# Attention and feed-forward block on one core: the first loads in one queue's order, six warming matmuls for eight, and two consecutive tokens to a row of a pair

## What is computed

```
x = x + softmax(q k^T / 8) v Wo + bo     q = layernorm(x) Wq, k = ctx Wk, v = ctx Wv; 8 heads of 64
y = silu((layernorm(layernorm(x)) * gamma + beta) W1 + b1)      W = (q - 128) * scales, groups of 128 rows
x = x + 0.5 * (y W2 + b2)                W1: 256 x 1024, W2: 1024 x 256
```

## Time and profile before

| | us |
|---|---|
| median of 3 runs | 188.02 (187.6 to 189.53) |
| profiled execution, its own time | 187.78 |
| its span | 186.0 |
| TensorE busy (matmul) | 180.9 |
| VectorE, ScalarE, GpSimd busy | 123.7, 123.2, 115.2 |

### The profile page before, as it was taken

One profiled execution on the slowest core, in us unless ns is written; L12 is line 12 of the kernel. 1 busy time (PEld: TensorE's weight loads), 2 busy tenths in 40 slices (PEclk: granted clock), 3 DMA queues, 4 the chain that ended last, 5 costly groups with the idle time before them and its releaser, 6 DMA issues.

```text
span 186.0 us, 3887 instructions
## 1 busy us (share of the span) xinstructions
PE 180.9 (97%) x1502; PEld 177.0 (95%) x1502; DVE 123.7 (67%) x261; ACT 123.2 (66%) x230; POOL 115.2 (62%) x159
## 2 busy tenths in 40 slices
PE   7999999899999999999999999999999999999994
PEld 7899789799999999999999999999999999999994
DVE  0189987999999374955496558847694768154341
ACT  3278752897967970898278935895289817962580
POOL 5021798997996984198708972597349762776220
PEclk9999999999999999999999999999999999999999
DMA  6998793000001000010001000100001000100101
GB/s 145 299 394 237 232 386 119 2 2 0 4 2 35 25 0 0 4 57 0 4 0 56 4 0 0 33 30 0 4 0 56 0 4 0 56 4 0 56 4 56
DMA packets 9480, 10.72 MB, mean 58 GB/s; under 512 B 2268, under 2 KB 8183, under 8 KB 9335
## 3 DMA queue, kind: packets, MB, share of 16 engines
q1 hardware_dynamic: 8981, 9.83, 16.3%
q10 hardware_dynamic: 482, 0.66, 1.3%
HBM read 8.38 MB, written 2.10 MB: 56 GB/s over the span
## 4 chain that ended last, share of the span: by engine, by line
PE 90%; DVE 6%; ACT 2%; issue 1%; POOL 0%
PE H L873 24%; PE T L887 21%; PE T L855 15%; PE S L834 14%; PE S L841 4%; PE S L784 4%; PE S L762 2%; DVE hT_hi L636 1%; PE T L817 1%; PE T L769 1%; PE H L769 1%; PE H L803 1%; PE S L803 1%; DVE smax L589 1%; DVE probs L596 1%; DVE hT_lo L638 1%
## 5 line engine op out<-in xcount | busy, mean ns | idle before, releaser
L315 POOL TENSOR_TENSOR y_lo<-y,y_hi 128x512 fp32r<-128x512 f32 x28 | 37.9, 1373 | 2.3 <-ACT y_hi L455 1.9
L873 PE MATMUL H<-hT_hi,w_hi 128*128 128x256 f32 x128 | 36.9, 288 | 0.8 <-DVE hT_lo L638 0.7
L281 POOL TENSOR_TENSOR probs<-probs,rsum 128x616 f32<-128x616 f32 x16 | 19.2, 1218 | 29.8 <-DVE rsum L608 29.8
L887 PE MATMUL T<-w_hi,y_hi 128*128 128x256 f32 x128 | 36.5, 285 | 0.0
L873 PE MATMUL H<-hT_lo,w_hi 128*128 128x256 f32 x128 | 35.5, 277 | 0.0
L873 PE MATMUL H<-hT_hi,w_lo 128*128 128x256 f32 x128 | 35.4, 277 | 0.0
L887 PE MATMUL T<-w_lo,y_hi 128*128 128x256 f32 x128 | 35.4, 277 | 0.0
L887 PE MATMUL T<-w_hi,y_lo 128*128 128x256 f32 x128 | 35.4, 276 | 0.0
L451 ACT ACTIVATE y<-H,vec 128x256 f32<-128x256 f32 x64 | 26.6, 469 | 7.0 <-PE H L873 7.0
L424 ACT ACTIVATE probs<-probs,rstd 128x616 f32<-128x616 f32 x16 | 12.8, 808 | 22.9 <-DVE probs L596 22.9
L873 PEld LDWEIGHTS H<-hT_hi,w_hi 128*128 128x128 f32 x128 | 24.1, 188 | 1.4 <-DVE hT_lo L638 1.4
(11 more groups left out here) (127 smaller groups left out, 459.2 us busy)
## 6 DMA issues: line engine op xcount, KB each, us to landing
q_sb<-in_L_ffn_fc_q SPq DMA_DIRECT2D x2, 1024.0 KB, 8.3
out_x<-x_sb SPq DMA_DIRECT2D x16, 128.0 KB, 1.8
x_sb<-in_x SPq DMA_DIRECT2D x7, 256.0 KB, 8.3
s_sb<-in_L_ffn_fc_scales SPq DMA_DIRECT2D x2, 512.0 KB, 12.6
s_sb<-in_L_ffn_fc_scales SPq DMA_DIRECT2D x1, 1024.0 KB, 7.8
wq_sb<-in_L_xattn_Wq SPq DMA_DIRECT2D x1, 512.0 KB, 6.3
wo_sb<-in_L_xattn_Wo SPq DMA_DIRECT2D x1, 512.0 KB, 8.6
wk_sb<-in_L_xattn_Wk ACTq DMA_DIRECT2D x1, 384.0 KB, 4.8
```

The source lines that it names most:

```text
L281: nc.gpsimd.tensor_tensor(p, p, rsum[:, j, :].unsqueeze(2).to_broadcast([P, HEADS, J]), ALU.mult).then_inc(norm_done, 1)
L315: nc.gpsimd.tensor_tensor(y_lo[:, two, :], y[:, two, :], f32(y_hi[:, two, :]), ALU.subtract).then_inc(y_lo_done, 1)
L873: ins = mm(r[:, q * W:(q + 1) * W], wt[:, c, m * P:(m + 1) * P], ht[:, c, :], start=c == q == i == 0, stop=c == q == 1 and i == 2)
L887: ins = mm(o, yt[:, m, j * P:(j + 1) * P], wt[:, m, :], start=m == 0 and i == 0, stop=m == M - 1 and i == 2)
```

## The change

It changes three things. All first loads are issued by SyncE in the order context, wk, wq, pair 0 of x, wv, wo, pair 1 of x, then as before; ScalarE keeps only the load of bo. The first group of warming matmuls has six in place of eight. Row p of a pair holds tokens 2p and 2p + 1 of the pair's 256, so that a pair is loaded as one run of 2 KB for each partition; the stores follow the same view.

```diff
-    x_v = x.rearrange("b s c -> (b s) c").rearrange("(n p) c -> p n c", p=P)
-    out_v = out.rearrange("b s c -> (b s) c").rearrange("(n p) c -> p n c", p=P)
+    x_v = x.rearrange("b s c -> (b s) c").rearrange("(a p j) c -> p a j c", p=P, j=UT)
+    out_v = out.rearrange("b s c -> (b s) c").rearrange("(a p j) c -> p a j c", p=P, j=UT)
...
                 sp.dma_start(ctx_sb[:, :, :], ctx_v).then_inc(ctx_in_sem, 16)
+                sp.dma_start(wk_sb[:, :, :], wk.rearrange("(n p) f -> p n f", p=CC)).then_inc(wk_in, 16)
                 sp.dma_start(wq_sb[:, :, :], wq.rearrange("(n p) f -> p n f", p=P)).then_inc(wq_in, 16)
+                sp.dma_start(x_sb[:, pair(0), :], x_v[:, 0, :, :]).then_inc(x_in[0], 16)
                 sp.dma_start(wv_sb[:, :, :], wv.rearrange("(n p) f -> p n f", p=CC)).then_inc(wv_in, 16)
                 sp.dma_start(wo_sb[:, :, :], wo.rearrange("(n p) f -> p n f", p=P)).then_inc(wo_in, 16)
-                sp.dma_start(x_sb[:, pair(1), :], x_v[:, pair(1), :]).then_inc(x_in[1], 16)
+                sp.dma_start(x_sb[:, pair(1), :], x_v[:, 1, :, :]).then_inc(x_in[1], 16)
...
-                        sp.dma_start(out_v[:, n:n + 1, :], x_sb[:, n:n + 1, :]).then_inc(stored, 16)
+                        sp.dma_start(out_v[:, f, j:j + 1, :], x_sb[:, n:n + 1, :]).then_inc(stored, 16)
...
             def _(act):
-                act.dma_start(wk_sb[:, :, :], wk.rearrange("(n p) f -> p n f", p=CC)).then_inc(wk_in, 16)
-                act.dma_start(x_sb[:, pair(0), :], x_v[:, pair(0), :]).then_inc(x_in[0], 16)
                 act.wait_ge(half_ready, 1)
...
                 pe.wait_ge(warm_ready, 1)
-                warm(8)
+                warm(6)
```

More of the change, by code:

```diff
@@ L231, in _ @@
                     sp.dma_start(s1_sb[:, c, :], s1[c:c + 1, :].to_broadcast([P, F])).then_inc(s1_in, 16)
-                sp.dma_start(x_sb[:, pair(2), :], x_v[:, pair(2), :]).then_inc(x_in[2], 16)
+                sp.dma_start(x_sb[:, pair(2), :], x_v[:, 2, :, :]).then_inc(x_in[2], 16)
                 sp.dma_start(b2_half[:, :], b2.rearrange("(o e) -> o e", o=1).to_broadcast([P, D])).then_inc(b2_in, 16)
@@ L246, in _ @@
                 for a in range(3, NA):
-                    sp.dma_start(x_sb[:, pair(a), :], x_v[:, pair(a), :]).then_inc(x_in[a], 16)
+                    sp.dma_start(x_sb[:, pair(a), :], x_v[:, a, :, :]).then_inc(x_in[a], 16)
                 for f in range(NA):
```

## The result

The changed kernel takes 189.05 us (median of 20 runs, 187.49 to 189.81), the kernel before in the same rounds 187.78 (20 runs, 186.95 to 189.67). The ratio is 1.0057, interval 1.0037 to 1.0077: 0.6% slower, where I had forecast no change and a range up to 188.9. Ratios leave out runs more than 1.5% above the fastest of the same kernel (none in this result, three of twelve in the run with six warmings in the kernel before), while medians and counts of runs leave out none. The spread matters more than usual: 10 of the 20 runs are over 189 us, against 3 of 20 before.

The account below looks back on a forecast made before the run. TensorE, busy 180.9 of 186.0 us, was taken to bound the kernel through the end of V. Of the front's 0.65 us, 0.55 is given back waiting for wv: 187.78 - 0.10 = 187.7 us, range 186.8 to 188.9.

Parts of the forecast that it names:

- The frame: TensorE bounds the kernel; whatever moves the end of V moves the kernel's end, and what doesn't move V is lost.
- Part 1: Two warming matmuls fewer before the context's transposes: warming loads end 0.87 us sooner, the transposes start 0.65 us earlier.
- TensorE slow for longer: Rival: with less warming the clock rises only at 9.0 us, V comes 1.1 us late, 188.9 us; chance 0.12.
- The context's landing: Context load ahead of its transposes: lands near 4.15 us, transposes at 4.25, 0.65 us earlier; bounds none and 1.25 us.
- Part 2: wk loaded behind the context: lands at 5.3 us, just in time for K at 5.44.
- Part 3: x0 behind wq, wv behind x0: wv lands at 9.31 us and gates V at 9.41, a gain of 0.10 us.
- the front's gain goes through whole: Rival: wv lands by 8.8 us, V starts at 8.86 without waiting, 187.1 us; chance 0.25.
- the rival's condition: wv landed at 8.8 us or before, so that V needn't wait for it.
- Parts 4 and 5: SyncE's longer queue, s1 issued 0.9 us later, costs nothing; token order in loads and stores 0, bounds -0.1 and +0.6 us.

## Why the prediction was wrong

**The frame held.** "Whatever moves the end of V moves the end of the kernel": over profiled executions with an early or a late rise, two queues or one (us),

| kernel | V starts | span | difference |
|---|---|---|---|
| before | 9.51 | 186.0 | 176.5 |
| changed, first profile | 11.39 | 187.7 | 176.3 |
| changed, second profile | 9.25 | 185.5 | 176.3 |
| changed, eight warmings | 9.63 | 185.9 | 176.3 |
| before, six warmings | 11.23 | 187.5 | 176.3 |
| changed, four warmings | 10.49 | 186.8 | 176.3 |
| before, tokens only | 9.29 | 185.6 | 176.3 |

The five others with x0 ahead of V give 176.3 or 176.4. The two with V ahead of x0 give 176.8 and 177.3, since there make_m doesn't stand right behind V; what makes the two differ by 0.5 us is open.

**Part 1 failed, and decided the case.** I priced the two warmings as 0.87 us that TensorE no longer spends, let K and all behind it run at the upper level as before, and so put at nothing in the sum what the warmings were there for; a rival with the chance 0.12 was all it got. Two warmings fewer in the kernel before, with nothing else changed, cost 0.85% (0.45 to 1.25%); given back in the changed kernel they take its ratio from 1.0057 to 1.0013. In the trace the change loses 1.88 us at V: it is 0.62 ahead when K starts, and the stretch from there to V takes 5.92 us in place of 3.42. The rival that I had written down, TensorE slow for longer, is what happened, and its formula holds: 5.47 + 3.42 + (10.6 - 5.47) / 2 = 11.5, measured 11.39. Its size was off as well: I had put the rise off to 9.0 us, and it came near 10.6; hence 1.9 us in that profiled execution in place of 1.1. The median, a mixture of runs with different rises, lost 1.27 us and stands 0.15 above the range. The Trainium skill ("TensorE: Matmul & The Clock Gate", What's actually happening) says that the number of slow matmuls differs from run to run; the trace agrees: one program, K's loads at 337 ns until 9.2 us in one profile, at 188 from some 5.6 us in the other. The spread of the runs before, which I had quoted for the rival (187.6 to 189.53), deserved more weight. That its long runs were late rises is likely but not shown, as none of them was traced; a late wv can make such a run too.

The context's landing, the term I spent most care on, was mis-sized too: its transposes start at 3.55, not 4.25, right behind the warming, and with four warmings even at 3.05. The front won 1.35 us there where I had 0.65 and a bound of 1.25, and K, waiting for wk until 5.47, kept 0.62 of it. The idle stretch that I had put ahead of the transposes (0.6 us) opened ahead of K's loads instead, 0.77 us in the first profile and 0.23 in the second.

**Part 2 was right in what bounds K, and lucky in its time.** wk landed at 5.43 (5.3 predicted), and K started at 5.47 (5.44), bound by it. In the second profile K started at 4.92, bound by it too: in the profiles with one queue wk took 3.4 to 4.3 us from its issue, and the first had one of the longest.

**Part 3 was right where the rise is early.** V began at 9.63 (eight warmings) and 9.25 (the change's second profile), behind a wait for wv of 0.41 and 0.61 us (9.41 and 0.55 predicted). In the first profile, with the late rise, wv landed 6.9 us after its issue at 2.6, and V at 11.39 didn't wait for it. The rival that the front's gain goes through whole is refuted for these runs by the gaps. So is the time that I had worked out from the Trainium skill's rule ("DMA: Bandwidth & Descriptors", Anatomy of one DMA — SWDGE (gpsimd) path), wv in before 7 us: by issue and time to landing, wv came at 8.7 to 11.2 us wherever it stood behind x0 in one queue. Where Part 3 was incomplete is this spread: at 8.7 (four warmings) wv met the rival's condition, at 11.2 it held V back until 11.28.

**Parts 4 and 5 cost nothing, as predicted.** GpSimd's first product for w1, which had waited for s1, waits for ScalarE in the changed kernel; the first line is of the kernel before, the others of the changed one:

```profile
18.12 2.53 POOL L320 TENSOR_TENSOR q_sb<-q_sb,s_sb 128x512 f32<-128x512 f32 x2 [5.59 <-DMA s_sb<-in_L_ffn_fc_scales]
...
18.93 2.54 POOL L323 TENSOR_TENSOR q_sb<-q_sb,s_sb 128x512 f32<-128x512 f32 x2 [4.53 <-ACT q_sb L465]
23.68 2.39 POOL L284 TENSOR_TENSOR probs<-probs,rsum 128x616 f32<-128x616 f32 x2 [2.22 <-DVE rsum L609]
```

s1 was issued 0.8 us later, but landed no later: its two parts took 11.5 and 13.6 us from issue to landing before, 10.5 and 11.3 after. The token order by itself has the ratio 1.0014 (0.9977 to 1.005) and leaves the last store at 2.1 us.

**What stays open.** Why a run rises early or late. What TensorE did before doesn't settle it. Four profiles with eight warmings and one queue have the same load starts to 0.02 us up to 5.2 us, and rise near 5.6, 6.4, 6.4 and 10.6 us; four with six warmings have the same starts up to 3.9 us, and rise near 4.0, 5.5, 7.2 and 10.6. So the number and the place of the warmings shift how often the rise is late, and don't fix it in a single run. The counts over 189 us fit this (nine matmuls split by the longer idle stretch 6 of 12, nine with none or almost none 1 and 3 of 12, seven 10 of 20), but they mix late rises with late loads. How amount and idle time share the effect I have not separated.

## What to carry to other kernels

Matmuls that compute nothing are not free to remove: price them by what the following instructions cost at the slower level, here 1.9 us in a run with a late rise and 1.3 us of median, for two removed at 0.87 us, and look at the spread of the runs before you trim them. Judge such a trim by many runs, since one profile can show either level. If a faster front only opens a wait, removing warming for it wins nothing. And when loads are put in a better order, sum the bytes up to the load whose consumer bounds the chain: if that set is the same, expect no gain; here none could be told.

## What the runs showed of the hardware

- TensorE's level can be read from single weight loads (mostly 333 to 338 ns for 128 columns of float32 against 186 to 193; 286 to 289 for the first of a slow group) where the granted clock column reads 1.00 throughout, and the trace's clock records begin only at the rise (10.6 and 5.5 us in the two profiles of the changed kernel).
- The rise came between 3.9 us (the token order alone, eight warmings) and 10.6 us, for kernels that differ by a few matmuls, and 5 us apart for the same program.
- A context load of 115.5 KB, issued 0.5 us ahead of the next load on one queue, let its reader start at 3.05 us (four warmings); with wk's load issued on the other queue at the same moment, readers started at 4.90, 4.29, 4.48 and 4.83.
- wv's load, with the same bytes ahead of it in one queue, landed from 8.7 to 11.2 us.
